# A quarter of the column terms of a graph network from matrix products on one Trainium2 core

## The chip, the cores and the metric

The kernel runs on one core of a Trainium2 chip. The metric is the device time of the whole program in microseconds (us); for the kernel before it is the median of three runs. TensorE is PE in the profile, VectorE is DVE, ScalarE is ACT, GpSimd is POOL, and SyncE (SP) only issues DMAs.

## The reference

A graph network with three layers over 12,500 nodes of 64 features and 200,000 edges, whose `src` and `dst` are drawn at random and then sorted by `dst`. The attention of an edge reads two nodes: its row node and its column node.

```
for l in range(3):
    f1 = relu(x[row] @ nb_W[l] + nb_b[l]);  f2 = relu(x[col] @ self_W[l] + self_b[l])
    h = relu(concatenate([f1, f2], axis=1) @ att1_W[l] + att1_b[l])
    mask = clip(sigmoid(h @ att2_W[l] + att2_b[l]) * 1.5 - 0.45, 0, 1)
    d = clip((segment_sum(mask, row) + 1e-6) ** -0.5, 0, 10)
    x = segment_sum((mask * d[row] * d[col])[:, None] * x[col], row);  out = out + x
return layernorm(x_in + out)
```

## The kernel before

Both halves of `h` are linear in what a node has, so each layer first makes two tables over the nodes (the **node phase**): P for the row side, kept in SBUF as `p_all` (104 blocks of 128 nodes, 64 wide), and Q for the column side, stored with x beside it to the DRAM table `qx_table`. An edge then needs the sum of one row of P and one of Q. The edges are sorted once at the start (the **setup**, until about 612 us): a bitonic sort on DVE, ending with L988 to L1009, which split the sorted keys into row lanes, column numbers and, for each tile of 128 edges, the block of P that its rows lie in. There are 1,664 tiles, in 208 groups of 8, in 52 quads of 4 groups.

**Phase A** of a layer makes the mask of every edge, group by group:

- POOL fetches Q and x of the 1,024 column nodes of a group with 8 indirect DMAs (L526) into one of four buffers `got[j]` (two of them are named `k_hot` and `g_hot` in the profile).
- DVE builds two sets of row one-hots, `hot_a` and `hot_b`, with 8 compares each (`build_hot`, L1047 to L1057). PE transposes `hot_a` (`turn_hot`, L643), ACT copies the result to `onehot_t` (`keep_turned`, L783), and PE multiplies it with blocks of P (`row_terms`, L646 to L654). The block numbers are data, so PE's sequencer loads 8 of them into registers (L648) and forms an address before each product.
- DVE adds the two terms (L1073), takes relu and the product with the attention vector (L1075), sums over the features (L1078), and forms the mask in small steps (L1080 to L1091) with one ACT exponential (L798) between them.
- PE adds the masks to the row sums, with `hot_b` as weights (L552).
- Beside this ACT makes the one-hots of the column lanes that the next phase needs (`make_look`, L785), from a broadcast that SP loads (L405); SP stores them, the row one-hots and x (L416, L420, L425).

**Phase B** uses the masks and the stored one-hots for the weighted sum. The change touches it only where its sums are cleared. Each engine runs its own list of instructions in order; what joins them are semaphores written by hand, so the order in the functions is the order on the engine. `onehot_t`, `hot_a`, `hot_b`, `hidden` and the two banks of `row_terms` have two buffers each.

## Time and profile before

| | us |
|---|---|
| median of three runs (9091.9 to 9094.2) | 9091.96 |
| span of the profiled execution | 9111.0 |
| PE busy (62%) | 5650.8 |
| DVE busy (74%) | 6736.5 |
| ACT busy (40%) | 3666.1 |
| POOL busy (65%) | 5960.7 |

The profiled execution has one time, its span, and it is the one beside which durations are added up; it is 19 us longer than the median. The first layer's phase A ends at about 2740 us; phase A of the second layer begins at about 3490 us. Busy time counts data instructions alone: loads of registers, address arithmetic and waits show as idle time of an engine, and where the profile names no releaser it calls this "issue". A one-line view of one source line does show loads of registers.

### The profile page before, as it was taken

What the parts mean: (1) busy time and instruction counts of PE and PEld (TensorE: products, weight loads), DVE (VectorE), ACT (ScalarE), POOL (GpSimd) and SP (SyncE); (2) the same over time, 40 slices, a digit from 0 to 9 for tenths busy, and PEclk for the clock granted to TensorE, in tenths of its full rate; (3) what the DMA queues carried; (4) which work ended last, traced back from release to release, by engine and by line L of the source; (5) the groups of instructions that cost most, each with busy time, mean ns of one, the idle gap of its engine ahead of it and who ended that gap; (6) DMA issues with size and microseconds to landing.
All of it is one profiled execution on the core that took longest, in us unless ns stands there. A gap on an engine that the chain in (4) does not pass through costs nothing.

```text
span 9111.0 us, 203370 instructions
## 1 busy us (share of the span) xinstructions
PE 5650.8 (62%) x43467; PEld 5151.5 (57%) x43630; DVE 6736.5 (74%) x29039; ACT 3666.1 (40%) x8663; POOL 5960.7 (65%) x6294
## 2 busy tenths in 40 slices
PE   3135555555558996555555557998555555555996
PEld 1135555545548885555555556887555555555886
DVE  8877777777777877777777777877777777776788
ACT  0013322322227883322322325885322322323886
POOL 0017777777775656777777776665777777776664
PEclk7565555555558996555555557998555555555998
DMA  1014444444456664444444446665444444445665
GB/s 24 0 48 135 132 130 131 132 130 130 133 128 206 213 206 130 132 131 130 132 130 131 132 130 176 210 212 156 132 130 130 133 130 131 132 130 146 213 211 161
DMA packets 1122388, 1272.27 MB, mean 140 GB/s; under 512 B 648596, under 2 KB 652724, under 8 KB 1122356
## 3 DMA queue, kind: packets, MB, share of 16 engines
q1 hardware_dynamic: 922676, 903.51, 32.1%
q0 software_dynamic: 199680, 368.45, 16.7%
q14 instruction: 26, 0.21, 0.0%
q8 instruction: 6, 0.10, 0.0%
HBM read 868.11 MB, written 403.23 MB: 140 GB/s over the span
## 4 chain that ended last, share of the span: by engine, by line
POOL 44%; issue 23%; PE 22%; DVE 8%; DMA 1%; ACT 1%; POOLq 0%; DVEq 0%; ACTq 0%; SPq 0%
POOL got L526 22%; PE bank L552 12%; POOL k_hot L526 11%; POOL g_hot L526 10%; PE bank L685 6%; DVE acc L946 2%; DVE acc L947 2%; PE bank L653 1%; PE bank L690 1%; PE bank L610 1%; PE bank L601 1%; PE bank L576 1%; DMA k_x<-kept_x 1%; DMA k_hot<-qx_table,index 0%; DVE acc L909 0%
## 5 line engine op out<-in xcount | busy, mean ns | idle before, releaser
L653 PE MATMUL bank<-p_all,onehot_t 128*128 x10032 | 2301.5, 424 | 1752.4 <-issue 1731.8
L653 PEld LDWEIGHTS bank<-p_all,onehot_t 128*128 128x128 f32 x10032 | 2186.8, 330 | 1803.4 <-issue 1803.4
L526 POOL DMA_INDIRECT got<-qx_table,index x2496 | 2376.4, 952 | 784.9 <-issue 780.3
L539 POOL DMA_INDIRECT got<-y_table,index x1248 | 1187.3, 951 | 798.8 <-issue 431.5
L798 ACT ACTIVATE small<-small 128x8 f32<-128x8 f32 x624 | 130.2, 209 | 3813.9 <-DVE small L1080 3813.9
L526 POOL DMA_INDIRECT k_hot<-qx_table,index x1248 | 1181.3, 947 | 393.7 <-issue 377.5
L526 POOL DMA_INDIRECT g_hot<-qx_table,index x1248 | 1185.6, 950 | 380.6 <-issue 380.6
L552 PE MATMUL bank<-mask,onehots 128*128 128x3 bf16 x4992 | 669.8, 184 | 986.1 <-DVE mask L1091 986.1
L552 PEld LDWEIGHTS bank<-mask,onehots 128*128 128x128 bf16 x4992 | 516.0, 104 | 1250.7 <-issue 1145.5
L1118 DVE SCALAR_TENSOR_TENSOR p_all<-iota_b,col_hi,bank 128x104 f32<-128x104 bf16 x3768 | 953.9, 317 | 341.5 <-PE bank L685 335.4
L1056 DVE TENSOR_SCALAR onehots<-iota_b,rows_b 128x128 bf16<-128x128 bf16 x5016 | 888.7, 280 | 48.0
L1056 DVE TENSOR_SCALAR onehots<-iota_b,rows_now 128x128 bf16<-128x128 bf16 x5040 | 891.0, 279 | 22.6
L783 ACT CAST onehot_t<-bank 128x1024 f32<-128x1024 bf16 x630 | 637.6, 1012 | 574.2 <-PE bank L643 534.4
L818 ACT ACTIVATE k_x<-k_x,k_weight 128x64 f32<-128x64 f32 x2496 | 630.1, 335 | 308.0 <-DMA k_x<-kept_x 204.5
L685 PE MATMUL bank<-d,onehot_t 128*128 128x104 bf16 x11376 | 615.7, 212 | 133.4 <-issue 106.6
L1073 DVE TENSOR_TENSOR bank<-bank,got 128x512 f32<-128x512 f32 x312 | 218.3, 700 | 633.6 <-DMA got<-qx_table,index 628.7
L643 PE MATMUL bank<-ident_b,onehots 128*128 128x128 bf16 x5040 | 667.3, 314 | 9.8 <-DVE onehots L1056 9.8
L685 PEld LDWEIGHTS bank<-d,onehot_t 128*128 128x128 bf16 x11376 | 562.2, 100 | 173.9 <-issue 92.5
L643 PEld LDWEIGHTS bank<-ident_b,onehots 128*128 128x128 bf16 x5040 | 631.4, 164 | 10.3 <-DVE onehots L1056 10.3
L1133 DVE TENSOR_TENSOR acc<-acc,bank 128x512 f32 x627 | 427.6, 682 | 79.1 <-issue 72.9
L1075 DVE SCALAR_TENSOR_TENSOR hidden<-bank,a_cur 128x512 f32<-128x512 f32 x624 | 431.4, 691 | 21.4
L1078 DVE TENSOR_REDUCE small<-hidden 128x8 f32<-128x512 f32 x624 | 428.1, 686 | 21.2
(167 smaller groups left out, 8859.7 us busy)
## 6 DMA issues: line engine op xcount, KB each, us to landing
onehot_t<-look_hot SPq DMA_DIRECT2D x474, 256.0 KB
row_hot<-onehots SPq DMA_DIRECT2D x468, 256.0 KB, 3.6
k_x<-col_rows SPq DMA_DIRECT2D x318, 256.0 KB, 3.6
kept_x<-got SPq DMA_DIRECT2D x312, 256.0 KB
look_hot<-k_x SPq DMA_DIRECT2D x312, 256.0 KB, 2.1
hot_in<-row_hot SPq DMA_DIRECT2D x312, 256.0 KB
k_x<-kept_x SPq DMA_DIRECT2D x312, 256.0 KB
look_new<-row_hot SPq DMA_DIRECT2D x159, 256.0 KB
```

The lines of the kernel that those rows point to most:

```text
L526: pool.indirect_dma_start(got[j][:, k, :], None, qx_table, bass.IndirectOffsetOnAxis(ap=index[j][:, k:k + 1], axis=0)).then_inc(a_got[j], 16)
L539: pool.indirect_dma_start(got[j][:, k, 0:HID], None, y_table, bass.IndirectOffsetOnAxis(ap=index[j][:, k:k + 1], axis=0)).then_inc(g_got[j ...
L552: return mm(to, lhsT, rhs, start=False, stop=True, skip_group_check=True)
L643: last = turn(bank_t[:, k, :], hot_a[j][:, k, :], ident_b[:, :])
L653: last = mm(bank_p[h][:, k, :], onehot_t[h][:, k, :], p_all[:, ds(ids[k], 1), :].rearrange("p o d -> p (o d)"), start=True, stop=True)
L685: last = mm(bank_d[n % 3][:, e, 0:NB], look_t[i % 3][:, q * (U // 2) + e, :], d3[:, s, :], start=(s == 0), stop=(s == 2))
L783: a.copy(onehot_t[h][:, :, :], bank_t).then_inc(a_trc, 1)
L818: last = a.activation(to[:, k, 0:HID], rows[:, k, 0:HID], ACT.Copy, scale=by(k))
L1056: last = v.tensor_scalar(to[:, k, :], iota_b[:, :], rows[:, k:k + 1], None, ALU.is_equal)
L1075: link(v.scalar_tensor_tensor(out=hidden[h][:, :, :], in0=bank_p[h], scalar=0.0, in1=a2_cur[:, :].unsqueeze(1).to_broadcast([PARTS, U, HID ...
L1078: link(v.tensor_reduce(sm[:, 0, :], hidden[h][:, :, :], AX.X, ALU.add), e)
L1118: last = v.scalar_tensor_tensor(out=picked[:, e, :], in0=iota_b[:, 0:NB], scalar=col_hi[:, ds(at + e, 1)], in1=bank_d[(2 * i + q) % 3][:, ...
```

## The change

In each quad the last group no longer gathers. Setup counts, for every group of sorted edges, its runs of equal column block within a tile, and puts the 52 groups with the fewest runs last in the quads; it then lists for each of them up to 72 runs in 9 rounds of 8 slots (`slot_words`: two addresses for each slot; `slot_lanes`: 128 column lanes for each slot, shifted so that lanes of other runs match nothing).

In phase A, DVE makes the one-hots of a round from a broadcast row of `slot_lanes` (`build_slots`), and PE multiplies each with a block of Q, held in SBUF as three bf16 parts side by side (`q3`, 192 wide), and adds it into `bank_q`, four banks that a quad clears once (`column_terms`). The row terms of that group are added into the same banks, and DVE sums the parts with one reduction in place of the add. Three rounds lie in each of groups 0, 1 and 2 of the quad. The transposed row one-hots of all groups are made by DVE from a broadcast of row lanes (`build_turned`), without PE and ACT, and the straight ones by one wide compare (`build_hot`). The node phase makes the three parts of Q on DVE, ACT and POOL. The sums that phase B adds to are cleared by one POOL memset instead of ACT copies; the weights of a layer are loaded by SP instead of copied by POOL.

```diff
+ def load_slots(b, r, made):
+     if made is not None:
+         sp.wait_ge(x_made, l * (ROUNDS * QUADS) + (b * ROUNDS + made))
+         sp.sem_inc(sp_go, 1)
+     sp.dma_start(slot_in[r % 3], slot_lanes[ds(b * SLOTS + r * U, U), :].rearrange("k e -> (k e)")
+                  .partition_broadcast(PARTS)).then_inc(x_in[r % 3], 16)
+ def load_rows(b, i):
+     h = i % 2
+     if not isinstance(b, int):
+         sp.wait_ge(a_trc, l * (GROUPS + 1) + (b * 4 + (i - 1)))
+         sp.sem_inc(sp_go, 1)
+     sp.dma_start(rows_in[h].rearrange("p k m -> p (k m)"), row_rows[ds((b * 4 + i) * U, U), :]
+                  .rearrange("t e -> (t e)").partition_broadcast(PARTS)).then_inc(a_rowin[h], 16)
...
  with sp.Fori(0, QUADS) as b:
      for j in range(3):
+         if j == 0:
+             sp.wait_ge(x_used[0], l * (slots_used(0) * QUADS) + b * slots_used(0))
+             sp.sem_inc(sp_go, 1)
+             sp.dma_start(slot_word[0:1, :], slot_words[ds(b, 1), 1, :]).then_inc(w_in, 16)
+             for r in range(3):
+                 load_slots(b, r, 0 if r == 0 else None)
+         load_rows(b, j + 2)
          load_columns(b, j + 2)
+         if j < 2:
+             for r in (3 * j + 3, 3 * j + 4):
+                 load_slots(b, r, r - 2)
          sp.wait_ge(a_got[j], (l * QUADS + b + 1) * GOT)
          sp.sem_inc(sp_go, 1)
          sp.dma_start(kept_x[ds((b * 3 + j) * PARTS, PARTS), :].rearrange("p (k d) -> p k d", k=U),
+         if j < 2:
+             load_slots(b, 3 * j + 5, 3 * j + 3)
+         else:
+             load_rows(b, 5)
...
+            for i in range(PICKS):
+ pool.indirect_dma_start(
+     picked_rows[i // CHUNK][:, i % CHUNK * PARTS:(i % CHUNK + 1) * PARTS], None, node_rows,
+     bass.IndirectOffsetOnAxis(ap=pick_row[:, i:i + 1], axis=0)
+ ).then_inc(s_picked[i // CHUNK], 16)
...
-     for j in range(4):
-         pool.wait_ge(a_idx[j], l * (QUADS + (j < 3)) + (b + 1))
+     for j in range(3):
+         pool.wait_ge(a_idx[j], l * (QUADS + 1) + (b + 1))
          pool.sem_inc(pool_go, 1)
...
+ pool.wait_ge(m_rows, l + 1)
+ pool.sem_inc(pool_go, 1)
+ pool.memset(acc[:, :, :], 0.0).then_inc(k_zero, 1)
...
- def turn_hot(j, g):
-     pe.wait_ge(a_hot, l * (GROUPS + 2) + (g + 1))
-     pe.wait_ge(a_trc, l * (GROUPS + 2) + g)
-     for k in range(U):
-         last = turn(bank_t[:, k, :], hot_a[j][:, k, :], ident_b[:, :])
-     last.then_inc(a_tr, 1)
+ def clear(to):
+     return mm(to[:, :], zeros_b[:, 0:PARTS], zeros_b[:, :], start=True, stop=True, skip_group_check=True)
  def row_terms(h, g, *read):
      pe.load(blk[h], block_of[0:1, ds(g * U, U)])
      ids = [pe.snap(r, min_val=0, max_val=BLOCKS - 1) for r in blk[h]]
-     pe.wait_ge(a_trc, l * (GROUPS + 2) + (g + 1))
-     pe.wait_ge(*read)
+     pe.wait_ge(a_trc, l * (GROUPS + 1) + (g + 1))
+     if read:
+         pe.wait_ge(*read)
      for k in range(U):
-         last = mm(bank_p[h][:, k, :], onehot_t[h][:, k, :],
-                   p_all[:, ds(ids[k], 1), :].rearrange("p o d -> p (o d)"), start=True, stop=True)
+         p_block = p_all[:, ds(ids[k], 1), :].rearrange("p o d -> p (o d)")
+         if read:
+             last = mm(bank_p[h][:, k, :], onehot_t[h][:, k, :], p_block, start=True, stop=True)
+         else:
+             last = plus(q_parts[:, k, 0:HID], onehot_t[h][:, k, :], p_block)
      last.then_inc(a_p, 1)
+ def column_terms(b, j):
+     n = l * QUADS + b
+     if j == 0:
+         for i in range(4):
+             pe.wait_ge(q_lo[i], stores(l + 1, (0, i)))
+         pe.wait_ge(w_in, (n + 1) * 16)
+         pe.sem_inc(pe_go, 1)
+     for r in range(3 * j, 3 * j + 3):
+         pe.load(q_at + k_at, slot_word[0:1, 2 * U * r:2 * U * (r + 1)])
+         pe.wait_ge(x_made, n * ROUNDS + (r + 1))
+         for i in range(U):
+             of = pe.snap(q_at[i], min_val=0, max_val=(NB - 1) * Q_COLS)
+             to = pe.snap(k_at[i], min_val=0, max_val=(U - 1) * OUT_COLS)
+             last = plus(bank_q[:, ds(to, Q_COLS)],
+                         slot_hot[r % 2][:, i * PARTS:(i + 1) * PARTS],
+                         q3_flat[:, ds(of, Q_COLS)])
+         last.then_inc(x_used[r % 2], 1)
- with pe.Fori(0, GROUPS // 2) as b:
-     for j in range(2):
-         g = b * 2 + j
-         row_terms(1 - j, g + 1, a_sum, l * GROUPS + g)
-         turn_hot(j, g + 2)
-         at = [pe.snap(r, min_val=0, max_val=BLOCKS - 1) for r in blk[j]]
-         pe.wait_ge(a_hotb, l * (GROUPS + 1) + (g + 1))
+ with pe.Fori(0, QUADS) as b:
+     for j in range(4):
+         g = b * 4 + j
+         if j == 2:
+             column_terms(b, j)
+             row_terms(1, g + 1)
+         else:
+             row_terms(1 - j % 2, g + 1, a_sum, l * GROUPS + g)
+         if j == 0:
+             pe.wait_ge(a_sum, l * GROUPS + g)
+             for i in range(4):
+                 clear(bank[4 + i])
+         if j < 2:
+             column_terms(b, j)
+         at = [pe.snap(r, min_val=0, max_val=BLOCKS - 1) for r in blk[j % 2]]
+         pe.wait_ge(a_hot, l * (GROUPS + 1) + (g + 1))
          pe.wait_ge(a_m3, l * GROUPS + (g + 1))
          for k in range(U):
-             last = plus(bank_r[:, ds(at[k] * 4, 3)], hot_b[j][:, k, :], mask3[j][:, k, :])
+             last = plus(bank_r[:, ds(at[k] * 4, 3)], hot[j % 2][:, k, :], mask3[j % 2][:, k, :])
...
+ def split_middle(s, j):
+     act.wait_ge(q_left, l * NODE_STEPS + (s + 1))
+     a.copy(q3[:, of_step(s), 1, :], q_rest[j]).then_inc(q_mid, 1)
...
- def keep_turned(h, g, picked_up):
-     act.wait_ge(a_tr, l * (GROUPS + 2) + (g + 1))
-     act.wait_ge(a_p, l * (GROUPS + 1) + picked_up)
-     a.copy(onehot_t[h][:, :, :], bank_t).then_inc(a_trc, 1)
...
-         keep_turned(j % 2, g + 2, g + 1)
          if j < 3:
              make_look(b, j)
-         to = (j + 3) % 4
-         act.wait_ge(a_add[to], l * QUADS + (b + (j > 0)))
-         if to < 3:
-             act.wait_ge(a_kept[to], (l * QUADS + (b + (j > 0))) * 16)
-         a.copy(index[to][:, :], col_id[:, ds((g + 3) * U, U)]).then_inc(a_idx[to], 1)
+         if j > 0:
+             to = j - 1
+             act.wait_ge(a_add[to], l * QUADS + (b + 1))
+             act.wait_ge(a_kept[to], (l * QUADS + (b + 1)) * 16)
+             a.copy(index[to][:, :], col_id[:, ds((g + 3) * U, U)]).then_inc(a_idx[to], 1)
...
+            link(v.tensor_scalar(moved, done, HI_AT, None, ALU.logical_shift_right))
+            link(v.tensor_tensor(starts[:, 1:COLS], moved[:, 1:COLS], moved[:, 0:COLS - 1], ALU.not_equal))
+            link(v.memset(starts.rearrange("p (t e) -> p t e", e=PARTS)[:, :, 0:1], 1.0))
+            link(v.tensor_reduce(runs, starts.rearrange("p (h e) -> p h e", h=2), AX.X, ALU.add))
+            link(v.scalar_tensor_tensor(out=kk, in0=runs, scalar=float(ALL_GROUPS), in1=group_key, op0=ALU.mult, op1=ALU.add))
...
+            for r in range(ROUNDS):
+ eight = picks[:, 0, r * U:(r + 1) * U]
+ link(v.max(eight, pair[r % 2]))
+ link(v.match_replace(pair[(r + 1) % 2], eight, pair[r % 2], 0.0))
...
-            v.tensor_scalar(lane_row, lane_keys, ROW_AT, 2 * PARTS - 1, ALU.logical_shift_right, ALU.bitwise_and)
-            v.tensor_scalar(lane_lo, lane_keys, PARTS - 1, None, ALU.bitwise_and)
+            v.tensor_scalar(lane_row, lane_keys, 2 * PARTS - 1, None, ALU.bitwise_and)
+            v.tensor_scalar(lane_lo, lane_keys, COL_AT, PARTS - 1, ALU.logical_shift_right, ALU.bitwise_and)
...
+     q_out = bank[4 + j % 2][:, :].rearrange("p (b d) -> p b d", d=HID)
+     v.tensor_copy(q3[:, of_step(s), 0, :], q_out).then_inc(q_hi, 1)
+     dve.wait_ge(q_lo[j], stores(l, (b, j)))
+     dve.wait_ge(q_hi, l * NODE_STEPS + (s + 1))
+     v.tensor_tensor(q_rest[j], q_out, q3[:, of_step(s), 0, :], ALU.subtract).then_inc(q_left, 1)
+     v.tensor_copy(got[j][:, :, 0:HID], q_out).then_inc(n_q, 1)
...
- def build_hot(to, rows, g, n, free, signal, stored=None):
-     v.tensor_copy(rows[:, :], row_lo[:, ds(g * U, U)]).then_inc(a_rows, 1)
-     dve.wait_ge(*free)
+ def build_hot(h, g, stored=None):
+     dve.wait_ge(a_row, l * (GROUPS + 1) + g)
      if stored is not None:
-         dve.wait_ge(stored[0], stored[1] * 16)
-     dve.wait_ge(a_rows, l * (2 * GROUPS + 3) + (n + 1))
-     for k in range(U):
-         last = v.tensor_scalar(to[:, k, :], iota_b[:, :], rows[:, k:k + 1], None, ALU.is_equal)
-     last.then_inc(signal, 1)
+         dve.wait_ge(*stored)
+     build_onehot(hot[h], row_lo[:, ds(g * U, U)]).then_inc(a_hot, 1)
+ def build_turned(h, g, loaded):
+     dve.wait_ge(a_rowin[h], (l * (GROUPS // 2 + 1) + loaded) * 16)
+     if not isinstance(g, int):
+         dve.wait_ge(a_p, l * (GROUPS + 1) + (g - 1))
+     v.tensor_scalar(onehot_t[h][:, :, :].rearrange("p k m -> p (k m)"),
+                     rows_in[h].rearrange("p k m -> p (k m)"), part_f[:, :], None,
+                     ALU.is_equal).then_inc(a_trc, 1)
+ def build_slots(b, r):
+     h = r % 2
+     dve.wait_ge(x_in[r % 3], (l * (3 * QUADS) + (b * 3 + (r // 3 + 1))) * 16)
+     dve.wait_ge(x_used[h], l * (slots_used(h) * QUADS) + (b * slots_used(h) + r // 2))
+     v.tensor_scalar(slot_hot[h], slot_in[r % 3], part_f[:, :], None, ALU.is_equal).then_inc(x_made, 1)
-         build_hot(hot_a[h], rows_a[h], g + 2, g * 2 + 3, (a_tr, l * (GROUPS + 2) + (g + 1)), a_hot)
+         if j < 3:
+             build_slots(b, 3 * j)
+             build_slots(b, 3 * j + 1)
+         build_turned(1 - h, g + 1, b * 2 + (j + 1) // 2 + 1)
          dve.wait_ge(a_p, l * (GROUPS + 1) + (g + 1))
-         dve.wait_ge(a_got[j], (l * QUADS + (b + 1)) * GOT)
-         v.tensor_tensor(bank_p[h], bank_p[h], got[j][:, :, 0:HID], ALU.add).then_inc(a_add[j], 1)
-         dve.wait_ge(a_add[j], l * QUADS + (b + 1))
-         link(v.scalar_tensor_tensor(out=hidden[h][:, :, :], in0=bank_p[h], scalar=0.0,
+         terms = bank_p[h]
+         if j < 3:
+             dve.wait_ge(a_got[j], (l * QUADS + (b + 1)) * GOT)
+             v.tensor_tensor(terms, terms, got[j][:, :, 0:HID], ALU.add).then_inc(a_add[j], 1)
+             dve.wait_ge(a_add[j], l * QUADS + (b + 1))
+         else:
+             terms = hidden[h][:, :, :]
+             v.tensor_reduce(terms, q_parts[:, :, 0:Q_COLS].rearrange("p k (s d) -> p k d s", s=PARTS_OF),
+                             AX.X, ALU.add).then_inc(a_parts, 1)
+             dve.wait_ge(a_parts, l * QUADS + (b + 1))
+         link(v.scalar_tensor_tensor(out=hidden[h][:, :, :], in0=terms, scalar=0.0,
                                      in1=a2_cur[:, :].unsqueeze(1).to_broadcast([PARTS, U, HID]),
                                      op0=ALU.max, op1=ALU.mult), e)
          link(v.tensor_reduce(sm[:, 0, :], hidden[h][:, :, :], AX.X, ALU.add), e)
+         if j < 3:
+             build_slots(b, 3 * j + 2)
...
-         build_hot(hot_b[1 - h], rows_b[1 - h], g + 1, g * 2 + 4,
-                   (a_row, l * (GROUPS + 1) + (g + 1)), a_hotb,
-                   (a_hotst[0], l * (2 * QUADS) + (b * 2 + (j + 1) // 2)) if h else (a_hotst[1], l * QUADS + (b + j // 2)))
+         build_hot(1 - h, g + 1, (a_hotst[j - 1], (l * QUADS + (b + 1)) * 16) if j else None)
```

On PE, a group before is one load, the 8 row products, the 8 transposes and the 8 products of the row sums:

```order
L648 TENSOR_LOAD block_of
L649 ISA
L653 ISA
L653 MATMUL bank<-p_all,onehot_t 128x64
...
L640 ISA
L643 MATMUL bank<-ident_b,onehots 128x128 x8
L665 ISA
L667 REGISTER_ALU
L552 ISA
L552 MATMUL bank<-mask,onehots 128x3
```

On PE, group 0 of a quad with the change (the products at L815, L704 and their ISA rows come 8 times each, and the round from L829 three times):

```order
L807 TENSOR_LOAD tile_at
L808 ISA
...
L815 ISA
L815 MATMUL bank<-p_all,onehot_t 128x64
L803 MATMUL bank_q<-zeros_b 128x512 x4
L825 REGISTER_ALU x2
L826 ISA
L829 TENSOR_LOAD slot_word
L830 ISA
L832 ISA
L704 MATMUL bank_q<-acc_q,k_hot 128x192
...
L855 ISA
```

The transposes are gone; the clears and three rounds stand between the row products and the wait for the mask (L855).

On DVE, the row one-hots before lie ahead of the add, and again behind the mask:

```order
L1056 TENSOR_SCALAR onehots<-iota_b,rows_now 128x128 x8
L1071 REGISTER_ALU
L1072 ISA
L1073 TENSOR_TENSOR bank<-bank,got 128x512
L1075 SCALAR_TENSOR_TENSOR hidden<-bank,a_cur 128x512
L52 ISA
L1078 TENSOR_REDUCE small<-hidden 128x8
L52 REGISTER_ALU
L1080 TENSOR_SCALAR small<-small,b_cur 128x8
```

On DVE, group 0 with the change:

```order
L1351 ISA
L1352 TENSOR_SCALAR k_hot<-hot_in,part_f 128x1024
...
L1343 TENSOR_SCALAR onehot_t<-onehots,part_f 128x1024
L1372 ISA
L1375 ISA
L1376 TENSOR_TENSOR bank<-bank,got 128x512
L1383 SCALAR_TENSOR_TENSOR hidden<-bank,a_cur 128x512
L52 ISA
L1386 TENSOR_REDUCE small<-hidden 128x8
...
L1352 TENSOR_SCALAR k_hot<-slot_in,part_f 128x1024
L1390 TENSOR_SCALAR small<-small,b_cur 128x8
```

Two slot one-hots and the transposed one-hots of the next group come ahead of the add; the third slot one-hots, with their waits (an ISA row at L1351), stand between the sum over the features and the mask.

## Rows read from the trace of the kernel before

**Rows 1.** Stretches: their length, PE's busy time and instructions, granted clock, DMA.

```profile
660.00:2500.00 1840.00, 1035.04 (x5925) 940.33 (x5924) 1316.65 (x5719) 547.43 (x834) 1390.73 (x1465) 0.50 0.47 131
2800.00:3400.00 600.00, 560.71 (x6674) 535.31 (x6722) 478.78 (x2689) 517.12 (x1728) 366.56 (x388) 0.99 0.68 210
```

**Rows 2.** Timeline of POOL in phase A: start, duration, operation, idle before.

```profile
1500.71 0.95 POOL L526 DMA_INDIRECT got<-qx_table,index  x1 [0.30 <-issue]
```

**Rows 3.** Timeline of DVE in one group of phase A.

```profile
1500.15 0.70 DVE L1073 TENSOR_TENSOR bank<-bank,k_hot 128x512 f32<-128x512 f32 x1 [2.63 <-DMA k_hot<-qx_table,index]
1501.61 0.69 DVE L1078 TENSOR_REDUCE small<-hidden 128x8 f32<-128x512 f32 x1
1502.33 0.23 DVE L1080 TENSOR_SCALAR small<-small,b_cur 128x8 f32<-128x8 f32 x1
...
1504.62 0.17 DVE L1091 TENSOR_TENSOR mask<-small,mask 128x8 bf16<-128x8 f32 x1
...
1504.94 1.39 DVE L1056 TENSOR_SCALAR onehots<-iota_b,rows_b 128x128 bf16<-128x128 bf16 x8
```

**Rows 4.** Timeline of PE: a group of phase A, then a piece of phase B.

```profile
1497.93 3.67 PE L653 MATMUL bank<-p_all,onehot_t 128*128 x16 [2.33 <-issue]
1501.39 1.06 PE L643 MATMUL bank<-ident_b,onehots 128*128 128x128 bf16 x8
1504.94 1.08 PE L552 MATMUL bank<-mask,onehots 128*128 128x3 bf16 x8 [2.48 <-DVE mask L1091]
```

```profile
3352.38 2.06 PE L552 MATMUL bank<-k_x,p_all 128*128 128x64 f32 x16
```

**Rows 5.** Views of L648, L693, L1166: register instructions, ns min/median/max.

```profile
L648 PEldq TENSOR_LOAD <-block_of x627: 1917/2222/3682, 669.0 to 8369.8; - x157
L648 PEldq FUSED_REGOPS  x312: 46/46/46, 681.2 to 8369.7; - x156
```

```profile
L693 PEldq TENSOR_LOAD <-spot_of x627: 587/591/1681, 2763.1 to 9050.8; - x157
L693 PEldq FUSED_REGOPS  x624: 66/66/80, 2772.0 to 9050.6; - x156
```

```profile
L1166 DVEq TENSOR_LOAD <-block_of x468: 282/287/308, 2768.4 to 9050.0; - x156
```

**Rows 6.** Groups by line and shape: busy us, mean ns of one, idle before.

```profile
L909 DVE TENSOR_SCALAR acc<-p_all,acc 128x1563 bf16<-128x1563 bf16 x98 | 61.7, 631 | 27.3 <-PE bank L552 21.9 <-DVE p_all L905 0.4
L941 DVE TENSOR_SCALAR acc<-acc 128x1024 f32<-128x1024 f32 x17 | 11.8, 694 | 0.6
L934 DVE TENSOR_TENSOR g_hot<-iota_b,row_lo 128x1024 f32<-128x1024 bf16 x156 | 191.4, 1227 | 4.0
```

**Rows 7.** Timeline of DVE: end of the setup, first steps of the node phase.

```profile
589.47 1.23 DVE L946 TENSOR_TENSOR acc<-acc 128x1024 f32<-128x1024 f32 x1
...
591.86 1.23 DVE L988 TENSOR_SCALAR acc<-acc 128x2048 int32<-128x2048 int32 x1
...
611.77 0.20 DVE L1017 COPY b_cur<-b_all 128x64 f32 x1 [0.24 <-DVE spot_of L1009]
...
618.03 0.69 DVE L1024 COPY got<-bank 128x512 f32<-128x512 f32 x1 [5.70 <-PE bank L610]
620.27 0.69 DVE L1024 COPY got<-bank 128x512 f32<-128x512 f32 x1 [1.55 <-PE bank L610]
```

**Rows 8.** The page's DMA queues: packets, MB, share of 16 engines' span.

```profile
q1 hardware_dynamic: 922676, 903.51, 32.1%
q0 software_dynamic: 199680, 368.45, 16.7%
```

**Rows 9.** Stretches of PE around the second phase A: busy (instructions), clock, DMA.

```profile
3470.00:3480.00 10.00, 10.00 (x58) 1.00 0.17 46
...
3490.00:3500.00 10.00, 6.85 (x47) 0.50 0.32 84
```

**Rows 10.** Timeline of DVE in phase B's start: eight steps together.

```profile
2754.46 7.56 DVE L1145 TENSOR_TENSOR x_cur<-x_cur,d_node 128x832 f32<-128x832 f32 x8
```

349 lines of the change are left out of this document (264 added, 85 removed).

## The prediction

> **What bounds the kernel now.** I read the table of stretches first. Phase A takes some 2,080 us of each layer and is even: in 1,840 us POOL is busy 1,390.7 us with 1,465 instructions, nearly all gathers, so one starts every 1,840 / 1,465 = 1.256 us [rows 1]. The timeline of POOL says the same from inside: 0.95 us for a gather and 0.30 us of issue before the next, without a wait for anybody [rows 2]. A quad has 4 x 8 = 32 gathers, which is 40.2 us, and 52 quads make 2,090 us. Then the timeline of DVE: it idles 2.63 us before L1073, released by the DMA of the gather [rows 3]. PE idles too [rows 4]. So POOL sets phase A's pace and everything else has slack; PE runs there at a granted clock of 0.50 (the lower level, 1.2 GHz), though it is busy for 56% of the stretch, while phase B shows 0.99 [rows 1]. Phases B and the node phase do not wait for phase A's engines and are left out of the sum except where named.
>
> **What the change takes from the bound.** 24 gathers instead of 32 put POOL's floor at 24 x 1.256 = 30.1 us a quad. If that were still the bound, phase A would shrink by 10.1 us in each of 156 quads. The question is what the chain through DVE and PE takes, which so far was hidden under 40.2 us.
>
> **Terms of that chain**, mask to mask (from the end of L1091 of one group to that of the next):
>
> - Row products, 16 instructions: 3.67 us at clock 0.5 [rows 4]. They stay.
> - Load of 8 block numbers. As int16 it is 2.22 us, and it is seen as the 2.33 us of issue ahead of L653 [rows 4, 5]. The change makes these words int32, like those of L693, at 0.59 us [rows 5]. This gain is in the sum.
> - Load of 16 int32 words ahead of each round. Not in the trace. Bounds: 0.59 us if length is free (L693), 2 x 2.22 = 4.4 us if it cost what L648's words do [rows 5]. A single word on DVE takes 0.29 us [rows 5], so from 1 to 8 words the cost is between a constant 0.24 us with 0.043 us a word, and a straight 0.074 us a word; 16 words are 0.94 or 1.18 us. I take 1.15 us, because type and engine are those of L693.
> - Addresses. A round's product needs an ISA row of some six register operations; three take 46 ns and a longer one 66 ns [rows 5], so about 80 ns. The 8 products of L552, each behind one ISA row, take 1.08 us at clock 0.5, about 0.125 us apart [rows 4]; with 0.03 us more each I take 0.157 us, 1.26 us for 8.
> - The array itself: 8 transposes of 128 columns take 1.06 us [rows 4], 0.107 us apart, so 192 columns take 0.16 us and 512 columns 0.43 us at this clock. A round is 1.3 us whichever limit holds, and the four clears 1.7 us.
> - DVE: slot one-hots, bf16 in and out, 1,024 wide. L909 takes 0.631 us for 1,563 wide in the same types, about 0.49 us when scaled down with a small constant; the upper bound is L934's 1.23 us for 1,024 [rows 6]. Transposed one-hots write fp32: 0.69 us, as L941 [rows 6], with the same upper bound. The straight one-hots take L934's form, 1.23 us, where 16 compares took 2 x 1.39 us [rows 3, 6].
> - Add 0.70, relu and product 0.70, sum 0.69 us; L1080 to the end of L1091 is 2.46 us [rows 3]. The reduction of 1,536 PSUM elements in group 3: 512 elements take 0.69 us [rows 3], so 1.8 us by length.
>
> **The sum at clock 0.5.** Group 0: from the mask, DVE makes the straight one-hots, two slots and the transposed ones (1.23 + 0.98 + 0.69 = 2.9 us); PE does the row products of the next group (3.7), the clears (1.7) and the first round (1.3). Only then is a slot buffer free for the third slot one-hots (0.5), behind which the mask's small steps are queued (2.5). With 0.4 us of semaphores this is 13.0 us. The add of the gathered terms lies beside the clears and costs nothing there. Group 1 has no clears: 11.3 us. Groups 2 and 3 together, from the mask of group 1: PE's row sums (1.3), three rounds at 1.15 + 0.1 + 1.26 = 2.5 us each (7.5), load and addresses (1.1), row products (3.7); DVE's reduction (1.8), relu and sum (1.4), small steps (2.5), semaphores (0.5): 19.8 us. Together **44.1 us a quad**, above POOL's 30.1 and above the 40.2 of before. Following the waits of both lists and of SP's one by one over several quads with these durations gives the same figure. Phase A: 156 x (44.1 - 40.2) = +608 us.
>
> One rule speaks for a dearer load. The Trainium skill, "Runtime: NRT & Kernel Launch", Instruction fetch mechanics, puts a TENSOR_LOAD at about 200 ns a register even in bulk. The rows do not agree for int32 (0.59 us for 8 words, 74 ns each) and exceed it for int16 (278 ns each) [rows 5]. By that rule the load of 16 would be 3.2 us, a quad about 63.6 us, and the whole about 12,860 us.
>
> **Other terms.** DMA: queue q1 moves 903.5 MB in 32.1% of the span, about 309 GB/s, and q0 368.5 MB in 16.7%, 242 GB/s [rows 8]. A quad after has about 6.5 MB on the first (13 new broadcasts of 256 KB are in it) and 1.6 MB on the second: 27.8 us of all engines, below 44.1. Hidden, but the transfers come in bursts behind SP's waits, so a late broadcast can hold a slot; if each took 8 us, the quad would take 49.0. SP has 14 DMAs and their waits more a quad; at about 0.4 us each they fit. ACT loses the copy to `onehot_t` and gains nothing in phase A.
>
> Setup: behind the sort come the ranking (11 us: four passes over 2,048, a few small products and steps), scatter and reload of the keys (11.5), splitting them (11.2), 9 rounds of a maximum and a replacement over 1,024 elements at 1.3 us each (L946's 1.23 us is the nearest row, [rows 7]) (23.5), slot words (2.6), a store and load (6), and 36 gathers at 1.256 us with three subtractions (49.5): 115.7 us, in place of the 19.9 us between 591.86 and 611.77 [rows 7]: **+96 us**. The bounds are +70 (transfers and steps overlap) and +130. Node phase: DVE has 2 more instructions of 0.69 us in each of 13 steps, whose pace is 2.24 us by PE [rows 7]; they fit, and the chain DVE, ACT, POOL at the end does not: +6 us a layer, **+18 us**. The memset on POOL in phase B's start lies beside DVE's 7.56 us at L1145 [rows 10]: nothing; without that cover some 7 us a layer.
>
> Total: 9,111 + 608 + 96 + 18 = 9,833 us of span; the median is 19 us below the span, so **9,815 us**.
>
> **Rivals.**
>
> *The clock rises or the chain is shorter: faster.* At full clock 16 row instructions of this shape take 2.06 us or less instead of 3.67 [rows 4], and clears and rounds halve. With loads of 1.15 us the quad is 40.6 us (9,270 us), still slower; with loads of 0.6 us it is 35.7 us: 9,111 + 114 - 702 - 19 = 8,504 us. The point from which it decides is a quad of 39.4 us, where the added 114 us are paid. For it: PE gets 6.7 us of unbroken work in group 0, more than before. Against it: the clock fell from 1.00 to 0.50 as phase A began [rows 9] and stayed there for 1,840 us with PE busy 56% [rows 1]. Full clock alone 5%; a quad below 39.4 us by clock, loads or more overlap 12%.
>
> *The gathers stay the bound.* 30.1 us a quad: 9,111 + 114 - 1,576 - 19 = 7,630 us. It needs PE and DVE to finish groups 0 to 3 in 30 us, while row products (14.7), rounds (11.7), clears (1.7) and row sums (4.3) alone are 32 us of PE. 4%.
>
> *Short loads at the low clock.* 0.6 us a round's load: 42.2 us, 9,518 us; 0.9 us: 43.0 us, 9,643 us. 14%.
>
> *Slow forms on DVE, or late broadcasts.* Slot one-hots at 1.23 us: 48.8 us a quad; broadcasts of 8 us: 49.0. Some 10,550 us. 11%.
>
> *Dear loads.* L648's price for 16 words: 70.8 us, about 13,980 us. 4%.
>
> *The forecast itself*, 43 to 46 us a quad: 50%.
>
> **How the numbers follow.** The likeliest is 9,815. Faster by over 0.2% (about what a measurement of this kernel can tell from no change) has 12 + 4 = 16%, the same 2%, slower 82%. For 8 in 10 the range runs from 8,950 (a quad of 38.5 us) to 10,560 (slow forms or late broadcasts); outside lie the full gain of the clock, the gather bound, and dear loads.
>
> **What would show each step.** POOL idle before gathers, released by ACT's `index`, would show that the gathers no longer bind. The load at L829 between 0.9 and 1.2 us, its three rounds before L815 in group 2 about 2.5 us apart, and PE's wait for the mask (L704 behind the `mask` line) gone from some groups show the PE terms; L1352 at 0.49, L1343 at 0.69 and L1130 at 1.23 us those of DVE. A granted clock well above 0.50 in phase A would make the forecast wrong towards faster; DVE idle before L1352 until a DMA, towards slower.

## The result and the profile after

The changed kernel takes 10,047.9 us (median of three runs, 10,047.6 to 10,050.9) against 9,092.0 us: 1.105 times the kernel before, 95% interval 1.103 to 1.107. It is slower, as forecast; the forecast was 9,815 us with a range of 8,950 to 10,560. The profiled execution has a span of 10,045.8 us.

From the page of the kernel before, the chain of work that ended last:

```profile
POOL 44%; issue 23%; PE 22%; DVE 8%; DMA 1%; ACT 1%; POOLq 0%; DVEq 0%; ACTq 0%; SPq 0%
```

The page of the kernel after, its busy times, its chain and its gathers (the answer to [rows 1] is in the next fence):

```profile
PE 7124.0 (71%) x50447; PEld 5879.3 (59%) x50448; DVE 6742.6 (67%) x20545; ACT 3030.4 (30%) x7874; POOL 5168.6 (51%) x5122
PE 54%; DVE 23%; issue 15%; DVEq 2%; DMA 2%; ACT 2%; POOL 1%; SPq 0%; ACTq 0%; POOLq 0%
L674 POOL DMA_INDIRECT got<-qx_table,index x2496 | 2533.1, 1015 | 2774.1 <-ACT index L989 2050.4
```

A stretch inside the first phase A of the kernel after, with the columns of [rows 1]:

```profile
760.00:2800.00 2040.00, 1438.48 (x7802) 1133.77 (x7800) 1262.03 (x3114) 355.95 (x592) 1116.42 (x1086) 0.55 0.63 179
```

POOL is no longer on the chain (1%, where it had 44% before) and sits idle before a gather until ACT has written the next indices: L989 comes behind DVE's add, so POOL now waits for the rest. The clock is 0.55, as low as in [rows 1] but for a little.

What a quad does on PE, in the timeline of the kernel after:

```profile
1505.18 3.67 PE L815 MATMUL bank<-p_all,onehot_t 128*128 x16 [1.71 <-DVE onehot_t L1343]
1508.64 1.91 PE L803 MATMUL bank_q<-zeros_b 128*128 128x512 bf16 x4
1510.35 2.65 PE L704 MATMUL bank_q<-acc_q,k_hot 128*128 x16
1513.81 1.31 PE L704 MATMUL bank_q<-acc_q,k_hot 128*128 x8 [0.81 <-issue]
1515.33 1.10 PE L704 MATMUL bank<-mask,onehots 128*128 128x3 bf16 x8 [0.21 <-issue]
1517.64 3.67 PE L815 MATMUL bank<-p_all,onehot_t 128*128 x16 [1.21 <-DVE onehot_t L1343]
1521.11 1.49 PE L704 MATMUL bank_q<-acc_q,k_hot 128*128 x8
1523.74 1.46 PE L704 MATMUL bank_q<-acc_q,k_hot 128*128 x8 [1.15 <-DVE k_hot L1352]
1526.19 1.48 PE L704 MATMUL bank_q<-acc_q,k_hot 128*128 x8 [0.99 <-issue]
1527.72 1.06 PE L704 MATMUL bank<-mask,onehots 128*128 128x3 bf16 x8
1530.03 1.46 PE L704 MATMUL bank_q<-acc_q,k_hot 128*128 x8 [1.25 <-issue]
1533.06 1.46 PE L704 MATMUL bank_q<-acc_q,k_hot 128*128 x8 [1.58 <-issue]
1535.52 1.46 PE L704 MATMUL bank_q<-acc_q,k_hot 128*128 x8 [1.00 <-issue]
1537.83 3.67 PE L704 MATMUL bank_q<-p_all,onehot_t 128*128 x16 [0.85 <-issue]
```

The three rounds ahead of the last row products start 3.0 and 2.5 us apart; the gaps marked "issue" are the loads of words. From the mask that ends before 1502.24 to the one before 1547.58 this quad is 45.3 us long. Over a layer, from its first mask (791.2) to its last (3125.2) by the trace, 207 steps of a group give 45.1 us a quad, 45.0 in the layers after; by the same count the kernel before has 40.0.

The register loads, answering [rows 5], from the views of L829 and L807, then of L829 in two short stretches:

```profile
L829 PEldq TENSOR_LOAD <-slot_word x1404: 1101/1112/2685, 782.5 to 9286.0; - x176
L807 PEldq TENSOR_LOAD <-tile_at x627: 587/597/1017, 774.8 to 9292.0; - x157
...
L829 PEldq TENSOR_LOAD <-slot_word x1: 1852/1852/1852, 1506.7 to 1506.7; - x1
L829 PEldq TENSOR_LOAD <-slot_word x1: 1101/1101/1101, 1524.8 to 1524.8; - x1
```

And DVE, answering [rows 3] and [rows 6], in the timeline of the same quad:

```profile
1503.40 0.87 DVE L1352 TENSOR_SCALAR k_hot<-hot_in,part_f 128x1024 bf16<-128x1024 bf16 x2
1504.20 0.74 DVE L1343 TENSOR_SCALAR onehot_t<-onehots,part_f 128x1024 f32<-128x1024 bf16 x1
...
1511.87 0.49 DVE L1352 TENSOR_SCALAR k_hot<-slot_in,part_f 128x1024 bf16<-128x1024 bf16 x1 [4.88 <-PE bank_q L704]
...
1525.20 0.17 DVE L1401 TENSOR_TENSOR mask<-small,mask 128x8 bf16<-128x8 f32 x1
...
1541.54 1.76 DVE L1380 TENSOR_REDUCE hidden<-bank_q 128x512 f32<-128x1536 f32 x1 [4.90 <-PE bank_q L704]
```

The prices are those of the sum: 0.49 us for a slot one-hots, 0.74 for the transposed ones, 1.76 for the reduction. The third slot one-hots wait 4.88 us for a buffer, and the mask is queued behind them.

Where the 934.8 us of span went (differences of the two traces, between the first and last mask of each layer, the copies that begin a layer and the first and last load of phase B, and the last load of phase B and the next layer's first mask):

| term | forecast, us | measured, us |
|---|---|---|
| three phases A | 608 | 783 |
| setup | 96 | 98 |
| node phases, up to the first mask | 18 | 21 |
| start of phase B (the memset) | 0 | 17 |
| rest of phase B | 0 | 15 |

The remaining 21 us of the miss of 233 are the profile's distance from the median, which was 19 us above it before and is 2 us below it now.

The start of phase B, in the timeline of the kernel after (L1453 is the L1145 of [rows 10]):

```profile
3126.97 6.07 POOL L683 MEMSET acc_q<- 128x7168 f32 x1 [34.90 <-PE bank L704]
3127.25 5.86 DVE L1408 TENSOR_SCALAR rows_sum<-rows_sum 128x104 f32<-128x104 f32 x1
...
3135.53 7.56 DVE L1453 TENSOR_TENSOR x_cur<-x_cur,d_node 128x832 f32<-128x832 f32 x8
```

### The profile page after: what moved, and what is told of

Read it like the earlier page. It is cut to its first block, busy times and chain, and to the rows that moved or that the text cites. A ratio compares the mean times of both kernels' runs of the same rounds, so it can differ in the third digit from the quotient of the medians.

```text
span 10045.8 us, 228264 instructions
## 1 busy us (share of the span) xinstructions
PE 7124.0 (71%) x50447; PEld 5879.3 (59%) x50448; DVE 6742.6 (67%) x20545; ACT 3030.4 (30%) x7874; POOL 5168.6 (51%) x5122
## 4 chain that ended last, share of the span: by engine, by line
PE 54%; DVE 23%; issue 15%; DVEq 2%; DMA 2%; ACT 2%; POOL 1%; SPq 0%; ACTq 0%; POOLq 0%
PE bank_q L704 21%; PE bank L704 11%; PE bank L815 11%; PE bank_q L875 5%; DVE k_hot L1352 4%; DVE hidden L1380 3%; PE bank_q L803 3%; DVE onehot_t L1343 2%; DVE acc_q L1142 2%; DVE acc_q L1143 2%; PE bank L803 1%; DVE hidden L1383 1%; DVE small L1386 1%; DMA slot_in<-slot_lanes 1%; DVE small L1390 1%
## 5 line engine op out<-in xcount | busy, mean ns | idle before, releaser
L704 PE MATMUL bank_q<-acc_q,k_hot 128*128 x11232 | 1954.6, 340 | 1086.2 <-issue 887.2
L704 PEld LDWEIGHTS bank_q<-acc_q,k_hot 128*128 128x128 bf16 x11232 | 1285.4, 115 | 1785.4 <-issue 1421.7
L815 PE MATMUL bank<-p_all,onehot_t 128*128 x7536 | 1705.8, 420 | 465.8 <-DVE onehot_t L1343 465.8
L815 PEld LDWEIGHTS bank<-p_all,onehot_t 128*128 128x128 f32 x7536 | 1622.9, 327 | 491.7 <-issue 491.7
L1426 DVE SCALAR_TENSOR_TENSOR p_all<-iota_b,col_hi,bank_q 128x104 f32<-128x104 bf16 x3768 | 953.1, 316 | 336.6 <-PE bank_q L875 331.1
L1352 DVE TENSOR_SCALAR k_hot<-slot_in,part_f 128x1024 bf16<-128x1024 bf16 x468 | 232.3, 496 | 1359.1 <-PE bank_q L704 1336.4
L704 PE MATMUL bank<-mask,onehots 128*128 128x3 bf16 x4992 | 567.8, 180 | 405.8 <-DVE mask L1401 370.1
L704 PEld LDWEIGHTS bank<-mask,onehots 128*128 128x128 bf16 x4992 | 463.4, 109 | 594.3 <-issue 507.9
L1130 DVE TENSOR_TENSOR onehots<-iota_b,row_lo 128x1024 bf16<-128x1024 bf16 x627 | 768.3, 1225 | 14.1
L875 PE MATMUL bank_q<-d,onehot_t 128*128 128x104 bf16 x11376 | 618.8, 212 | 146.8 <-issue 95.9
L875 PEld LDWEIGHTS bank_q<-d,onehot_t 128*128 128x128 bf16 x11376 | 565.3, 100 | 187.0 <-issue 109.5
L704 PE MATMUL bank_q<-p_all,onehot_t 128*128 x2496 | 572.5, 424 | 129.2 <-issue 118.7
L704 PEld LDWEIGHTS bank_q<-p_all,onehot_t 128*128 128x128 f32 x2496 | 544.0, 330 | 176.1 <-issue 176.1
L1352 DVE TENSOR_SCALAR k_hot<-hot_in,part_f 128x1024 bf16<-128x1024 bf16 x936 | 430.0, 489 | 71.0 <-PE bank_q L704 70.0
```

The lines of the kernel that those rows point to most:

```text
L704: return mm(to, lhsT, rhs, start=False, stop=True, skip_group_check=True)
L815: last = mm(bank_p[h][:, k, :], onehot_t[h][:, k, :], p_block, start=True, stop=True)
L875: last = mm(bank_d[n % 3][:, e, 0:NB], look_t[i % 3][:, q * (U // 2) + e, :], d3[:, s, :], start=(s == 0), stop=(s == 2))
L1130: return v.tensor_tensor(to[:, :, :], iota_b[:, :].unsqueeze(1).to_broadcast(wide), of.unsqueeze(2).to_broadcast(wide), ALU.is_equal)
L1352: v.tensor_scalar(slot_hot[h], slot_in[r % 3], part_f[:, :], None, ALU.is_equal).then_inc(x_made, 1)
L1426: last = v.scalar_tensor_tensor(out=picked[:, e, :], in0=iota_b[:, 0:NB], scalar=col_hi[:, ds(at + e, 1)], in1=bank_d[(2 * i + q) % 3][:, ...
```

## The experiments

Each kernel was profiled; its quad is given by the same count as above, from the first to the last mask of the first layer (45.1 us for the changed kernel). The first three and `e6` ran once, the others two to ten times. The kernel before, run beside them, took 9,096 to 9,110 us, against 9,092 us beside the changed kernel, so a difference of up to 18 us between two of these kernels can be that of the chips.

### What the rounds cost

The first three leave work out of the rounds. For `e1_no_word_loads`:

```diff
-                        pe.load(q_at + k_at, slot_word[0:1, 2 * U * r:2 * U * (r + 1)])
...
-                            last = plus(bank_q[:, ds(to, Q_COLS)],
+                            last = plus(bank_q[:, i * OUT_COLS:i * OUT_COLS + Q_COLS],
                                         slot_hot[r % 2][:, i * PARTS:(i + 1) * PARTS],
-                                        q3_flat[:, ds(of, Q_COLS)])
+                                        q3_flat[:, (r * U + i) * Q_COLS:(r * U + i + 1) * Q_COLS])
```

> The changed kernel with constant addresses in the column rounds: the 9 loads of 16 words and the address arithmetic of a quad are left out, so the column terms are those of wrong blocks; products, slot one-hots, broadcasts and all waits stay. My theory: in the changed kernel a quad of phase A takes 45.1 us because PE's list, with 9 loads of 1.1 to 1.8 us, alternates with DVE's. Following both lists with the durations of the changed kernel's trace, the quad falls by 3.6 us to about 41.5 us, the program to about 9,490 us. Rival, the loads are the one thing that keeps the chain above the gathers: a quad of 31 to 33 us, about 8,000 us. Rival, transfers or indices for POOL set the pace: no change, about 10,050 us.

Measured: 9,222.6 us, a quad of 39.7 us. The gathers did not become the bound (32 us would have), and the transfers were not it either; but the fall is 5.4 us where 3.6 were expected. Two things left the list that the expectation had not taken out: the address arithmetic of the products (68 ns each, 72 a quad), and some of the low clock, 0.62 in place of 0.55 over the same stretch. How the 1.8 us divide between them was not told apart.

For `e2_one_product` the inner loop became `for i in range(1)`, with the loads kept:

> The changed kernel with one column product in each round instead of 8: 63 of 72 products of a quad are left out (the column terms are incomplete), the loads of 16 words, one-hots, broadcasts and waits stay. My theory: 38 us a quad, about 8,990 us; then the alternation of DVE and PE over the row products (3.67 us), the third slot one-hots and the mask is what remains, still above POOL's 30.1 us. Rival, POOL becomes the bound as soon as PE is relieved: 30 to 31 us a quad, about 7,800 us.

Measured: 9,106.7 us, a quad of 38.9 us where 38 was expected. `e3_no_rounds` joins both edits:

> The changed kernel with neither loads nor products in the column rounds but one product with a constant address each, which only signals (the column terms are left out); one-hots, broadcasts and waits stay. My theory: almost the same as with one product and the loads, 38 us a quad and about 8,980 us, since the sequencer's loads then lie beside the row products. Rival, loads and products add up on one list: 3 to 5 us a quad less than with the loads kept, about 8,300 us.

Measured: 8,997.4 us, a quad of 38.2 us. Set against the changed kernel this is the telling run. Rounds that take PE about 22 us a quad cost 6.9 us of time; with nearly nothing in them the quad is still 8 us above the 30.1 us that the forecast gave POOL, and 6 us above what its 24 gathers take in this kernel, where they are 1.35 us apart. What is left can be read in the timeline of PE of this kernel:

```profile
1504.39 3.67 PE L815 MATMUL bank<-p_all,onehot_t 128*128 x16 [1.71 <-DVE onehot_t L1340]
1507.86 1.91 PE L803 MATMUL bank_q<-zeros_b 128*128 128x512 bf16 x4
1509.56 0.53 PE L704 MATMUL bank_q<-acc_q,k_hot 128*128 128x192 bf16 x2
1510.51 0.26 PE L704 MATMUL bank_q<-acc_q,k_hot 128*128 128x192 bf16 x1 [0.42 <-DVE k_hot L1349]
1513.31 1.09 PE L704 MATMUL bank<-mask,onehots 128*128 128x3 bf16 x8 [2.54 <-DVE mask L1398]
```

PE waits for DVE's one-hots, DVE for the row products and the round behind them, PE for the mask. In the stretch from 1500 to 2500 us PE is busy 574 us and DVE 733 us, so neither is full, and each stands idle for the other in turn.

### The order of waits

`e4_three_slot_buffers` gives the slot one-hots a third buffer, in a part of `q3` that no block uses:

```diff
+        slot_hot.append(q3_flat[:, BLOCKS * Q_COLS:BLOCKS * Q_COLS + U * PARTS])
...
-                        last.then_inc(x_used[r % 2], 1)
+                        last.then_inc(x_used[r % 3], 1)
```

> The changed kernel with three buffers for the slot one-hots instead of two, so that DVE need not wait for a round before it builds the third; all else is the same and complete. DVE shows some 9 us of waiting for such a buffer in each quad, behind which the mask is queued. My theory: PE's list is full by itself, so the quad falls by only 1.1 us, to about 9,870 us. Rival, those waits lie on the path in full: 36 us a quad, about 8,600 us.

Measured: 9,956.4 us, a quad of 44.5 us (1.0945 times the kernel before, 1.091 to 1.098). DVE's waits changed place, in the views of its waits between 1500 and 2500 us, first of the changed kernel, then of this one:

```profile
DVE k_hot L1352 <- PE bank_q L704: 197.4, 78, 4.9
DVE hidden L1380 <- PE bank_q L704: 112.1, 22, 5.7
...
DVE hidden L1381 <- PE bank_q L705: 182.6, 22, 8.9
DVE k_hot L1353 <- PE bank_q L705: 101.6, 90, 3.4
```

The waits ahead of the slot one-hots, the 4.88 us above among them, were halved, and what was gained there came back as a longer wait for PE ahead of the reduction. So they were worth 0.6 us a quad, about half of what was expected. `e8_rows_first` keeps the three buffers and moves PE's row products in group 2:

```diff
                         if j == 2:
-                            column_terms(b, j)
                             row_terms(1, g + 1)
+                            column_terms(b, j)
...
+                            dve.wait_ge(x_used[2], l * (slots_used(2) * QUADS) + (b + 1) * slots_used(2))
                             terms = hidden[h][:, :, :]
```

> The changed kernel with three slot buffers and, in group 2 of a quad, PE's row products ahead of its three column rounds (DVE's reduction then waits for the last round); complete. Theory: the loads of the rounds then run while the array works off the row products; following the lists the quad falls by 2.6 us against three buffers alone (44.5 us), to 41.9 us, about 9,550 us. Rival, the place of the row products does not matter since PE's list is as long: 44.5 us, about 9,950 us.

Measured: 9,545.4 us, a quad of 41.9 us (1.048, 1.046 to 1.050). Nothing was taken from the work; 2.6 us came from the order alone, as expected, but only in small part for the expected reason. From the views of PE's waits between 1500 and 2500 us, `e4` and then this kernel:

```profile
PE bank L705 <- DVE mask L1402: 50.5, 22, 2.3
...
PE bank L705 <- DVE mask L1403: 0.2, 1, 0.2
```

PE's idle time under "issue", which holds the loads of words, fell from 6.8 to 6.1 us a quad (added up from the same two views). The larger part is the wait of 2.2 us a quad for the mask of group 3, which is gone: DVE now makes that mask while PE does row sums and row products.

### The memset, the clock, the type of the block numbers

`e5_early_memset`:

```diff
-                pool.wait_ge(m_rows, l + 1)
+                pool.wait_ge(x_used[0], (l + 1) * (slots_used(0) * QUADS))
                 pool.sem_inc(pool_go, 1)
                 pool.memset(acc[:, :, :], 0.0).then_inc(k_zero, 1)
```

> The changed kernel with POOL's memset of the sums waiting for the last column round instead of for the last row sums; all else is the same and complete. In the changed kernel's trace DVE's L1408, which takes 0.21 us in the kernel before, lasts 5.86 us while POOL's memset of 6.07 us runs. Theory: the memset holds DVE up, and moved to a time when DVE waits for PE it costs nothing: 17 us less in three layers, about 10,031 us. Rival, L1408 is slow for another reason or the memset is hidden: no change, within 3 us of 10,048.

Measured: 10,029.9 us (10,026.5 to 10,041.3), 18 us less, on a chip where the kernel before takes 18 us more than beside the changed kernel, so the times alone do not price the step. The traces do: from the last mask of a layer to the first load of phase B, three layers together, this kernel takes as long as the kernel before, and the changed kernel 17 us more. From the view of L1408 of this kernel and its timeline of POOL:

```profile
L1408 DVE TENSOR_SCALAR rows_sum<-rows_sum x3: 214/214/215, 3122.3 to 9289.4; 128x104 f32<-128x104 f32 x3
...
3110.36 6.07 POOL L683 MEMSET acc_q<- 128x7168 f32 x1 [23.50 <-PE bank_q L704]
```

The memset is as long as before and L1408 is back at 0.21 us. The Trainium skill, "SBUF — State Buffer", Who interferes with whom, says that VectorE and GpSimd share a pair of ports as a lock, held for a whole instruction, and that the other engine stands still meanwhile when its own instruction is of a kind that uses them; these rows agree.

`e6_filled_array` adds products that only fill PE:

```diff
+                        for i in range(2):
+                            clear(bank[0])
                         pe.load(q_at + k_at, slot_word[0:1, 2 * U * r:2 * U * (r + 1)])
...
+                        for i in range(4):
+                            clear(bank[0])
                         at = [pe.snap(r, min_val=0, max_val=BLOCKS - 1) for r in blk[j % 2]]
```

> The changed kernel with more work for PE and nothing else changed: 2 products of 512 zero columns into an unused bank ahead of each load of words and 4 ahead of each wait for the mask, 34 a quad; results are complete. It prices the rival of the high clock. If the fuller array is granted full clock in phase A, the row products fall from 3.67 to 2.1 us and the quad by 2.7 us or, with the fillers' own time, by 0 to 2.7 us: 9,630 to 10,050 us. If the clock stays near 0.55, the fillers cost 0.43 us each, in part beside loads and waits: 50 to 58 us a quad, 10,800 to 12,000 us.

Measured: 10,016.6 us, a quad of 44.8 us. A stretch, and two rows of PE's timeline, of this kernel:

```profile
1500.00:2500.00 1000.00, 809.81 (x4583) 545.26 (x4583) 618.97 (x1535) 171.35 (x287) 545.10 (x538) 0.74 0.64 180
...
1504.87 3.67 PE L815 MATMUL bank<-p_all,onehot_t 128*128 x16 [1.35 <-DVE onehot_t L1347]
...
1511.87 0.82 PE L704 MATMUL bank_q<-acc_q,k_hot 128*128 x8
```

The mean clock rose to 0.74 and the time hardly moved. In this quad it is high in the rounds (8 products in 0.82 us, where 1.46 us is usual), which the loads of words pace anyway, and low in the row products (3.67 us). Over the first phase A, of 170 sets of row products that can be told apart, 44 took 1.8 to 2.3 us and 103 took 3.6 to 3.8, so the full clock reached only a quarter of them, and the fillers take time of their own. Filling the array this way gains nothing; what the full clock in all row products would give was not measured.

`e7_before_int32` changes the kernel before, in one word:

```diff
-        block_of = sb("block_of", [1, TILES + AHEAD], mybir.dt.int16)
+        block_of = sb("block_of", [1, TILES + AHEAD], I32)
```

> The kernel before with the block numbers kept as int32 instead of int16, nothing else. Theory: the load of 8 words ahead of the row products falls from 2.2 to 0.6 us, and the time does not change (within 0.2% of the kernel before), because POOL's gathers are the bound. Rival on the load: it is slow for its place in the list and stays at 2.2 us. Rival on the bound: the load lies on the path, up to 1.6 us in each of 624 groups, about 8,100 us.

Measured: 9,105.7 us, 0.9997 times the kernel before (0.9987 to 1.0006). The load, from the view of L648 of this kernel:

```profile
L648 PEldq TENSOR_LOAD <-block_of x627: 587/592/1166, 669.3 to 8351.8; - x157
```

The type made the 2.2 us of [rows 5]; and 1.6 us taken from PE in each group gave nothing where POOL is the bound.

### The rest of the change, and mixtures

`e9_all_gathered` drops `column_terms`, `build_slots` and the clears, and gives group 3 its gather, buffer and index back:

```diff
-                    for j in range(3):
-                        pool.wait_ge(a_idx[j], l * (QUADS + 1) + (b + 1))
+                    for j in range(4):
...
-                        if j == 0:
-                            pe.wait_ge(a_sum, l * GROUPS + g)
-                            for i in range(4):
-                                clear(bank[4 + i])
-                        if j < 2:
-                            column_terms(b, j)
```

> The changed kernel with the column terms undone alone: the last group of each quad gathers as in the kernel before, no slots, rounds or clears in phase A, while setup, the node phase and DVE's row one-hots from broadcasts stay as changed; complete. Theory: POOL is the bound again at 32 gathers, 40.2 us a quad, and the rest of the change costs its setup and small terms: about 9,300 us. Rival, what was changed around the row one-hots slows phase A by itself: more than 41 us a quad, above 9,420 us.

Measured: 9,530.4 us, a quad of 41.7 us. The rival holds: with POOL as the bound the rest of the change costs 1.7 us a quad. Between 1400 and 2500 us the gathers start 1.307 us apart, in the kernel before 1.253; times 32 that is the 1.7 us. In the timeline of POOL and DVE of this kernel:

```profile
1502.76 0.96 POOL L677 DMA_INDIRECT g_hot<-qx_table,index  x1 [0.30 <-issue]
1503.20 1.23 DVE L1138 TENSOR_TENSOR onehots<-iota_b,row_lo 128x1024 bf16<-128x1024 bf16 x1
1504.02 1.23 POOL L677 DMA_INDIRECT g_hot<-qx_table,index  x1 [0.30 <-issue]
1504.34 0.75 DVE L1351 TENSOR_SCALAR onehot_t<-onehots,part_f 128x1024 f32<-128x1024 bf16 x1
1505.56 0.95 POOL L677 DMA_INDIRECT k_hot<-qx_table,index  x1 [0.31 <-issue]
```

The first gather had begun when L1138, the straight one-hots, started, and takes 0.96 us as usual. The second begins while L1138 runs and takes 1.23 us: it ends 0.82 us after L1138 does. It is so throughout: of the 842 gathers between 1400 and 2500 us, 94 begin while L1138 runs, and just these are slow. They last 1.38 us on average (1.06 to 1.98), and each ends 0.83 us after L1138; no other gather lasts more than 0.98. They overlap L1351, the transposed one-hots, too, but only because that is the next instruction on DVE. The kernel before, with 8 small compares in place of L1138, has no gather above 0.98 us in the same stretch. Its wide compare of phase B (L934) does the same to the few gathers that meet it so: 15 gathers take up to 1.63 us.

`e10_every_second_quad` has the loops of all engines run over pairs of quads, the first of a pair without column terms and with four gathered groups:

```diff
-                with pe.Fori(0, QUADS) as b:
-                    for j in range(4):
+                with pe.Fori(0, HALF) as p:
+                    for b, has in ((p * 2, 0), (p * 2 + 1, 1)):
+                        for j in range(4):
...
-                        if j < 2:
-                            column_terms(b, j)
+                            if j < 2 and has:
+                                column_terms(p, j)
```

> The changed kernel with column terms in every second quad only; in the others all four groups gather (28 gathers a quad on average, a POOL floor of 35.2 us); two slot buffers, the order of the change, complete. Theory: PE's and DVE's long list of one quad is averaged with the short one of the next while POOL runs ahead within its buffers; following the lists gives 36.6 us a quad, about 8,730 us, faster than both kernels. Rival, POOL cannot run ahead by more than its buffers and each kind of quad takes its own bound, 45.0 and 40.2 us: 42.6 us, about 9,670 us.

Measured: 8,921.1 us, 0.981 times the kernel before (0.979 to 0.983), a quad of 37.8 us: faster than both, though slower than the 8,730 us expected. `e11_combined` adds the edits of e4, e8 and e5:

> Column terms in every second quad, together with three slot buffers, the row products ahead of the rounds in group 2 and the early memset; complete. Theory: 35.5 us a quad, where POOL's 35.2 us is the bound again: about 8,550 us. Rival, the quads with rounds keep their own bound (41.9 us) and the others 40.2 us: 41.0 us, about 9,410 us.

Measured: 8,855.5 us, 0.974 times (0.972 to 0.975), a quad of 37.4 us. POOL does run ahead, so the averages hold and not the bounds of each kind of quad. Both are 1.2 and 1.9 us a quad above the expectation, for the reason that e9 showed: gathers 1.35 us apart (e10) and 1.33 us (e11), times 28, are 37.8 and 37.3 us. In e11 POOL is the bound again, and the bound has grown.

`e12_turned_in_other_form` changes one instruction of e11:

```diff
-                    v.tensor_scalar(onehot_t[h][:, :, :].rearrange("p k m -> p (k m)"),
-                                    rows_in[h].rearrange("p k m -> p (k m)"), part_f[:, :], None,
-                                    ALU.is_equal).then_inc(a_trc, 1)
+                    v.tensor_tensor(onehot_t[h][:, :, :].rearrange("p k m -> p (k m)"),
+                                    rows_in[h].rearrange("p k m -> p (k m)"),
+                                    part_f[:, :].to_broadcast([PARTS, U * PARTS]), ALU.is_equal).then_inc(a_trc, 1)
```

> The combined kernel with one instruction changed: the transposed row one-hots come from a two-tensor compare (1.23 us, as the straight ones) instead of a compare with a scalar (0.75 us); complete. In the combined kernel and in the one that gathers in all groups, a gather that overlaps the scalar form lasts 1.3 us on average, others 0.95 us; in the kernel before, without such wide instructions, none is stretched. Theory: the wide scalar form on DVE holds POOL up for its length; with the other form DVE has 2 us more work a quad, but the gathers fall from 1.33 to about 1.28 us apart (the slot one-hots still stretch some), the quad from 37.4 to 36.1 us, the program to about 8,650 us. Rival, the gathers are stretched by traffic of the broadcasts on the DMA queues: no change in their length, the quad 37.4 us or more, 8,850 to 9,100 us.

Measured: 9,061.6 us, 0.995 times (0.994 to 0.997), a quad of 38.8 us: slower than e11, and neither theory. In its timeline:

```profile
1508.77 1.23 DVE L1144 TENSOR_TENSOR onehots<-iota_b,row_lo 128x1024 bf16<-128x1024 bf16 x1
1509.69 1.22 POOL L683 DMA_INDIRECT got<-qx_table,index  x1 [0.30 <-issue]
1510.70 1.22 DVE L1357 TENSOR_TENSOR onehot_t<-onehots,part_f 128x1024 f32<-128x1024 bf16 x1
1511.21 1.54 POOL L683 DMA_INDIRECT got<-qx_table,index  x1 [0.30 <-issue]
1513.06 0.96 POOL L683 DMA_INDIRECT got<-qx_table,index  x1 [0.30 <-issue]
```

The expectation had the wrong instruction. It read the overlap with the transposed one-hots (L1357) as the cause; what counts is which instruction DVE is in when a gather begins. The gather of 1509.69 begins in L1144, the straight one-hots, and that of 1511.21 in L1357; they end 0.91 and 0.83 us after these. Counted between 1400 and 2500 us:

| gathers that begin while DVE runs | e11: number, mean us | e12: number, mean us |
|---|---|---|
| the straight one-hots, L1144 | 113, 1.36 | 105, 1.49 |
| the transposed one-hots, L1357 | 45, 1.09 | 47, 1.56 |

In e11 the straight one-hots make 45 of the 54 us by which gathers are longer than 0.955 us in that stretch, the transposed ones 6. e12 lengthened the smaller source, from 0.75 to 1.22 us, and its share rose from 6 to 28 us (of 89). The gathers that overlap L1144 and stay at 0.96 us had begun before it. That the slow gathers are held by DVE, and not by traffic of the transfers, follows from their end: those that begin in L1144 end 0.86 us after it on average in both kernels, though L1357 takes 0.75 us in one and 1.22 us in the other. Two forms of compare do it, with a scalar and with two tensors; that the scalar form alone makes it is refuted. The Trainium skill's page "SBUF — State Buffer", named above, has both forms take shared ports, the scalar one in a fast mode and a two-tensor one with both inputs in SBUF; but it infers that the latter leaves the issuing of such gathers alone, and the 94 of 94 in e9 speak against that. The run that would follow, e11 with its straight one-hots made by the 8 small compares of the kernel before, was not made.

## Why the prediction was right, and where it was off

**The bound moves from POOL to the chain of PE and DVE.** Right, and the mechanism is shown: POOL idle until ACT's index, 1% of the chain, and e3 with 38.2 us a quad above POOL's floor, forecast at 30.1 us (32 us with the gathers as they run in that kernel).

**The prices.** All within a sixth: load of 16 words 1.11 us in most rounds (forecast 1.15, from [rows 5]), address arithmetic 68 ns (80), slot one-hots 0.49 (0.49), transposed 0.75 (0.69), straight 1.23 (1.23), reduction 1.76 (1.8), clears 1.91 with the last one's own length (1.7). But three or four loads of nine take over 1.4 us, mostly 1.5 to 1.85 (1506.7 above) and at most 2.7. Half of these run beside row products, half do not, and in e8 loads beside row products are no longer than the others; what makes them long stays open, and no row of before shows it.

**The sum.** 44.1 us a quad was forecast and 45.0 measured. Groups 0 and 1 came out shorter than forecast (12.4 and 10.8 us for 13.0 and 11.3); the step that failed is that of groups 2 and 3, 19.8 us forecast and 22.2 in this quad. It let PE's row sums and rounds start at the mask of group 1, at 1525.4. PE was then still in the third round of group 1, until 1527.7 (the rows at 1526.19 and 1527.72). The forecast treated groups 1 and 2 apart, though PE's list binds them. That is 2.3 of the 2.4 us; a long load in the three rounds (0.7 us) is made up for by smaller terms. That the quad came out within 1 us is in part luck, as groups 0 and 1 were put too long by 1.1 us. The quads that the rivals give for other prices of a load (42.2, 43.0, 63.6 and 70.8 us) do not follow from this sum, which has three loads of 16 words on the path; the following of the lists that is said to give them is not shown.

**The gain over 40.2.** The kernel before has 40.0 us a quad by the count used here: 0.2 of the 5.0 us. Its gathers start 1.253 us apart, where the forecast took 1.256.

**The memset at nothing.** Wrong. It was set beside DVE's 7.56 us at L1145 [rows 10]. It ran earlier, from 3126.97 to 3133.04 us, before that line began (L1453, at 3135.53), and beside L1408, which the first products of phase B wait for and which took 5.86 us. The price named for the case without cover, some 7 us a layer, was near: the start of phase B took 17 us more in three layers, and e5 took them back.

**What was not in the sum.** The rest of phase B took 15 us more, for a reason that no run shows. The stretched gathers were not foreseen either; they cost nothing while PE and DVE are the bound.

**Setup and node phases.** 98 for 96 us; 21 for 18 us. 50 us of the setup are the 36 gathers, forecast at 45: thirty have the price of [rows 2], six are longer.

**The rivals.** The high clock did not come by itself, and in e6 the fuller array brought clock but no time; its full price stays unmeasured, as the row products got little of it. Dear loads: refuted; 16 words in 1.10 us are 70 ns each. The Trainium skill's 200 ns a register ("Runtime: NRT & Kernel Launch", Instruction fetch mechanics) does not hold here; that page describes loads of registers from HBM, and these come from SBUF. Slow forms on DVE: refuted. Late broadcasts: refuted, as DVE waited for one 19 times in the whole run, 22.7 us in all. From the view of L1352 of the changed kernel:

```profile
  DMA slot_in<-slot_lanes: 22.7, 19
```

The gathers as the bound: only without column terms (e9) or with them in half of the quads (e10, e11).

## What to carry to other kernels

When work is moved off the bound, the new time is that of the chain that was hidden below it; follow that chain through both engines' lists before counting the gain, and take the work off only until the two are level: taking off a quarter of the gathers cost 10.5%, an eighth gained 1.9% and, with the order mended, 2.6%. Two engines that hand each other small pieces can both be idle a third of the time and still set the pace; order and buffers (e8, 3.2 us a quad) then give nearly half of what leaving out the work itself gives (e3, 6.9 us). An instruction placed beside other work on another engine is free only if that engine can go on while it runs. And of two instructions that overlap a slow one, the one that was running when it began is the first to suspect.

## What the runs showed of the hardware that was not expected

- A load of 8 register words takes PE 2.2 us from int16 and 0.59 us from int32 (e7). 16 words from int32 take 1.10 us, and three or four of nine loads over 1.4 us.
- A POOL memset of 6.07 us held a DVE instruction of 0.21 us for 5.86 us; moved to where DVE waits, it cost nothing (e5).
- A gather that POOL issues while DVE runs a wide one-hot compare ends 0.8 to 0.9 us after the compare does, so it takes up to 2.0 us in place of 0.95; one that had begun before the compare is not held. This moves a bound of 32 gathers from 40.0 to 41.7 us (e9), and more when a compare takes longer (e12). Eight small compares do not do it (no gather of 878 above 0.98 us in the kernel before).
- PE's granted clock rose from 0.55 to 0.74 with products that compute nothing, without any gain (e6).
